# Graph attention, expert routing and a sparse feed-forward network on one core: routing moved into the graph attention's program, the bias in one product

## The reference

```python
x = x + gat(ctx, adj=layernorm(x))        # two layers, 8 heads of 64, weights W0, W1, biases b0, b1, elu
x = x + moe(layernorm(x))                 # logits = xn @ gate_w.T; top 2 of 8 experts, softmax of the two
x = x + cross_attention(layernorm(x), ctx)
x = x + ffn_2to4(layernorm(x))            # silu gate, 2048 wide, two of four kept, down
# in gat:
e = leaky_relu(attn_self + attn_neigh) + -1e10 * (1 - adj)
out = softmax(e) @ feat + b
```

## Time and profile before

| | us |
|---|---|
| median of 3 runs (lowest, highest) | 1199.75 (1198.94, 1200.93) |
| time of the profiled execution | 1200.97 |
| its span in the profile | 1199.3 |
| PE busy (share of the span) | 981.4 (82%) |
| DVE busy | 663.5 (55%) |
| ACT busy | 375.0 (31%) |
| POOL busy | 274.7 (23%) |

### The profile page before, as it was taken

One profiled execution on the slowest core, in us unless ns is written; L12 is line 12 of the kernel. 1 busy time (PEld: TensorE's weight loads), 2 busy tenths in 40 slices (PEclk: granted clock), 3 DMA queues, 4 the chain that ended last, 5 costly groups with the idle time before them and its releaser, 6 DMA issues. The chain is left out here.

```text
span 1199.3 us, 15555 instructions
## 1 busy us (share of the span) xinstructions
PE 981.4 (82%) x4555; PEld 812.4 (68%) x4556; DVE 663.5 (55%) x1384; ACT 375.0 (31%) x624; POOL 274.7 (23%) x299
## 2 busy tenths in 40 slices
PE   4967423999999997433357799999999999999996
PEld 3744203999999996322245678888888888888885
DVE  7955557442253422676788754454556555555445
ACT  5844311332343322333333411222122222212220
POOL 0466002333132510446613200301020100201000
PEclk8987655999999999576677999999999999999998
DMA  8357104454153521442101100201011100100001
GB/s 336 70 117 167 71 2 141 154 174 145 64 178 120 162 74 45 126 134 60 44 1 53 54 1 1 71 1 35 0 35 35 35 0 0 35 0 1 36 36 70
DMA packets 35836, 86.36 MB, mean 72 GB/s; under 512 B 5840, under 2 KB 5968, under 8 KB 34512
## 3 DMA queue, kind: packets, MB, share of 16 engines
q1 hardware_dynamic: 27216, 62.76, 14.9%
q0 software_dynamic: 8576, 23.08, 7.7%
HBM read 63.01 MB, written 22.81 MB: 72 GB/s over the span
## 5 line engine op out<-in xcount | busy, mean ns | idle before, releaser
L72 PE MATMUL ps<-f_x_lo,f_w_hi 128*128 128x512 f32 x512 | 202.8, 396 | 13.9 <-POOL f_w_lo L1131 7.2
L73 PE MATMUL ps<-f_x_hi,f_w_lo 128*128 128x512 f32 x512 | 201.6, 394 | 0.0
L74 PE MATMUL ps<-f_x_hi,f_w_hi 128*128 128x512 f32 x512 | 201.4, 393 | 0.0
L1193 DVE TENSOR_TENSOR f_hid<-f_sg,ps 128x512 f32<-128x512 f32 x64 | 43.8, 686 | 196.9 <-ACT f_sg L1188 196.7
L72 PEld LDWEIGHTS ps<-f_x_lo,f_w_hi 128*128 128x128 f32 x512 | 97.6, 191 | 35.7 <-DVE f_hid L1193 7.2
L74 PEld LDWEIGHTS ps<-f_x_hi,f_w_hi 128*128 128x128 f32 x512 | 97.5, 190 | 20.7
L73 PEld LDWEIGHTS ps<-f_x_hi,f_w_lo 128*128 128x128 f32 x512 | 97.7, 191 | 20.4
L72 PE MATMUL ps<-gu_w_lo,m_xT_hi 128*128 (+1 forms) x312 | 106.2, 340 | 4.0 <-DVE m_xT_lo L1651 3.1
L1188 ACT ACTIVATE f_sg<-ps 128x512 f32<-128x512 f32 x64 | 38.3, 599 | 227.6 <-PE ps L74 227.4
L72 PE MATMUL ps<-f_w_lo,kv_c_hi 128*128 128x512 f32 x256 | 102.1, 399 | 5.4 <-DVE x L2248 5.4
L73 PE MATMUL ps<-f_w_hi,kv_c_lo 128*128 128x512 f32 x256 | 101.9, 398 | 0.0
(11 more groups left out here) (303 smaller groups left out, 1939.9 us busy)
## 6 DMA issues: line engine op xcount, KB each, us to landing
raw<-in_moe_gu SPq DMA_DIRECT2D x32, 352.0 KB
y_scratch<-m_y SPq DMA_DIRECT2D x39, 256.0 KB
raw<-in_ffn_gu SPq DMA_DIRECT2D x16, 512.0 KB, 3.5
raw<-in_moe_dn SPq DMA_DIRECT2D x24, 256.0 KB
x<-in_x SPq DMA_DIRECT2D x4, 1024.0 KB, 12.7
gat_rows<-g_ybuf SPq DMA_DIRECT2D x16, 256.0 KB
xn_scratch<-g_n_xn SPq DMA_DIRECT2D x16, 256.0 KB, 2.3
raw<-in_ffn_dn SPq DMA_DIRECT2D x16, 256.0 KB, 2.6
```

The costliest lines, as they stand in the source:

```text
L72: eng.matmul(out, lhs_hi, rhs_lo, start=start, stop=False)
L73: eng.matmul(out, lhs_lo, rhs_hi, start=False, stop=False)
L74: return eng.matmul(out, lhs_hi, rhs_hi, start=False, stop=stop)
L1193: dve.tensor_tensor(out, sg[:, k, :], self.UP[k], ALU.mult).then_inc(self.hid_made, 1)
```

## The change

1. **The route block is gone.** A new class `Rank` does its work inside `gat_rows`: the choice of experts batch by batch as the logits arrive (`dve_choose`), the exponentials likewise (`act_exp`), the counts by small float32 products per batch (`pe_count`), then weights, places and one-hot matrices once (`dve_weights`, `dve_places`), the token half of the one-hot products' operand by ACT in 17 operations (`act_tokens`), the 32 products, now behind two halves of `off_hot` (`pe_index`), and the table by a compare and a transpose. Running sums over tiles, some clamps and copies are gone.
2. **The first four gathers** (`gather_rows`) come ahead of the barrier, on POOL.
3. **The logits** are made by one float32 product instead of `product3`; so the transposed tiles are only copied (ACT; DVE for batch 3), and `gate_w` isn't split. The copies go into `c_raw` and `w_raw` in turn, so they wait for the sums over these (`cmax_made`, `wsum_made`). `XN` is 8 buffers instead of 4.
4. **The order in `gat_rows`**: PE transposes batch 0 and 1 behind all `features`; `act_norm` of batch 0 comes at step 15; POOL has `pool_rstd(0)` ahead of `second_arg(3)`; all stores of normalised tiles come behind the rows' stores.
5. **The check's bounds** use the largest attention values as one factor: the Abs on ACT, `scale_w` on POOL and four loads of 256 KB are gone; `weight_sums` reads `w_raw`. The limits are `GAP_MIN` 65536 and `BOUND_MAX` 16000 instead of 16384 and 4000.
6. **The bias** of the second layer takes one product: its high part stands in row 0 and its low part in row 32 of one operand, and the stationary matrix has ones in both rows.
7. **In `moe`**, expert 0's weights are split as the other experts' are: ACT's four copies, DVE's four differences, then the down weights. The gathered rows, their indices and semaphores live outside `moe`, and later stages reuse the rows' space.

```diff
-                    pe.matmul(bank, first[:, :], b1_lo[:, :], start=True, stop=False)
-                    pe.matmul(bank, first[:, :], b1_hi[:, :], start=False, stop=False)
+                    pe.matmul(bank, first[:, :], b1_parts[:, :], start=True, stop=False)
...
-                        if b == B - 1 and m == 2:
-                            pe.wait_ge(pool_const, 3)
-                            for i in range(3):
-                                norm.pe_turn(pe, i)
-                        if b == B - 1 and m == 3:
-                            norm.pe_turn(pe, 3)
                         features(b, m)
...
+                turn_batch(0)
+                turn_batch(1)
                 pe.wait_ge(y_made, T)
                 lo.pe_logits(pe, 0)
                 lo.pe_turn_logits(pe, 0)
+                lo.pe_logits(pe, 1)
+                turn_batch(2)
+                lo.pe_turn_logits(pe, 1)
+                lo.pe_logits(pe, 2)
+                rank.pe_count(pe, 0)
...
+                turn_batch(3)
+                lo.pe_turn_logits(pe, 2)
+                lo.pe_logits(pe, 3)
+                rank.pe_count(pe, 1)
+                rank.pe_count(pe, 2)
+                lo.pe_turn_logits(pe, 3)
+                rank.pe_count(pe, 3)
+                rank.pe_index(pe)
...
# POOL
+                rank.pool_const(pool)
                 second_arg(0)
                 second_arg(1)
                 add_rows(0)
                 second_arg(2)
                 add_rows(1)
+                lo.pool_rstd(pool, 0)
                 second_arg(3)
-                scale_w(0)
-                norm.pool_rstd_for_act(pool, 0)
                 add_rows(2)
-                scale_w(1)
-                norm.pool_rstd_for_act(pool, 1)
+                lo.pool_rstd(pool, 1)
                 add_rows(3)
...
+                lo.pool_rstd(pool, 2)
+                lo.pool_rstd(pool, 3)
+                rank.pool_gather(pool)
...
# DVE, behind the loop's step 12
+                    if t == 13:
+                        dve.tensor_reduce(cmax[:, :], c_raw[:, :, :], AX.XY, ALU.max,
+                                          apply_absolute_value=True).then_inc(cmax_made, 1)
+                    if t in (12, 14):
+                        stats((t - 12) // 2)
...
                 for k in range(DC):
                     weight_sums(k)
+                weight_sums(DC).then_inc(wsum_made, 1)
+                stats(2)
...
                 lo.dve_logits(dve, 0)
+                rank.dve_choose(chain, 0)
+                stats(3)
                 lo.dve_logits(dve, 1)
+                rank.dve_choose(chain, 1)
                 for i in range(TB):
+                    lo.dve_copy(dve, 3 * TB + i)
                 lo.dve_logits(dve, 2)
+                rank.dve_choose(chain, 2)
...
                 lo.dve_logits(dve, 3)
+                rank.dve_choose(chain, 3)
+                rank.dve_weights(chain)
+                rank.dve_places(chain)
+                rank.dve_tokens(chain)
```

More of the change, by code:

```diff
@@ new lines, in dve_stats @@
+    def dve_stats(self, chain, c):
+        for i in range(TB):
+            ins = chain.eng.bn_stats(self.st[:, i, :], self.X[:, TB * c + i, :])
+        chain.link(ins)
+        for i in range(TB):
+            ins = chain.eng.bn_aggr(self.mv[:, TB * c + i, :], self.st[:, i, :])
+        chain.link(ins)
+        s = slice(TB * c, TB * c + TB)
+        chain.eng.tensor_scalar(self.ve[:, s], self.mv[:, s, 1], EPS, None, ALU.add).then_inc(self.var_ready, 1)
+        chain.eng.tensor_scalar(self.nmean[:, s], self.mv[:, s, 0], -1.0, None, ALU.mult).then_inc(self.var_ready, 1)
@@ L211, in act_norm @@
         if t >= self.XN:
+            act.wait_ge(self.turned, t - self.XN + 1)
             act.wait_ge(self.xn_stored[t % self.XN], 16 * (t // self.XN))
-        self.norm.act_norm(act, t)
-    def act_hi(self, act, t):
-        c, i = divmod(t, TB)
[L217 to L223, removed]
+        act.activation(self.xn[:, t % self.XN, :], self.X[:, t, :], ACT.Identity, bias=self.nmean[:, t:t + 1],
+                       scale=self.rstd[:, t:t + 1]).then_inc(self.xn_ready, 1)
@@ new lines, in pe_turn, with turned_tile @@
+    def pe_turn(self, pe, t):
+        bank = self.turn_banks[t % self.BANKS]
+        pe.wait_ge(self.xn_ready, t + 1)
+        if t >= self.BANKS:
+            pe.wait_ge(self.x_copied[(t - self.BANKS) // TB], (t - self.BANKS) % TB + 1)
+        for d in range(DC):
+            ins = pe.transpose(bank[:, P * d:P * d + P], self.xn[:, t % self.XN, P * d:P * d + P], self.ident[:, :])
+        ins.then_inc(self.turned, 1)
+    def turned_tile(self, eng, t):
+        c, i = divmod(t, TB)
+        eng.wait_ge(self.turned, t + 1)
+        if i == 0 and c >= 2:
+            eng.wait_ge(self.lg_done, c - 1)
+        return (self.x_t[c % 2][:, :, P * i:P * i + P],
+                self.turn_banks[t % self.BANKS].rearrange("p (d n) -> p d n", d=DC))
@@ L1415, in sb @@
             return ctx.enter_context(nc.sbuf_tensor("m_" + name, shape, dt))
[L1417 to L1419 removed]
+        rows, got = rt["rows"], rt["got"]
         xT_hi = sb("xT_hi", [P, 2, DC, P], F32R)
@@ L1635, in _ @@
                 act.sem_inc(y_done, 2)
+                split(0, slice(0, 1), range(DC))
                 rows_hi(0, 0)
+                act.wait_ge(ld_dn, 16 * RE)
+                act.copy(rt["dn_w_hi"][:, 0], rt["raw_dn"]).then_inc(dn_hi, 1)
                 act_silu(0, 0)
@@ L1720, in sb @@
             return ctx.enter_context(nc.sbuf_tensor("a_" + name, shape, dt))
-        pair = [sb(f"pair{k}", [P, D]) for k in range(2 * TB)]
+        pair = [rt["rows"][:, k, :] for k in range(TB)] + [sb(f"pair{k}", [P, D])[:, :] for k in range(TB)]
         x_hi = sb("x_hi", [P, 2, DC, N], F32R)
@@ L2293, in build @@
             "lg": sb("logits", [P, T, E]),
+            "rows": sb("moe_rows", [P, 4, D]),
+            "index": [sb(f"moe_index{k}", [P, 1], I32) for k in range(4)],
+            "spacer": sb("moe_spacer", [P, 1]),
+            "got": [sem(f"e_got{k}") for k in range(4)],
+            "index_ready": sem("e_index_ready"),
             "xn_dram": nc.dram_tensor("xn_scratch", (B * N, D), F32, kind="Internal").ap(),
```

691 lines of the change are left out of this document (347 added, 344 removed).

## The result

The changed kernel takes 1160.03 us (median of 4 runs, 1158.97 to 1162.02) against 1200.08 in the runs beside it: a ratio of 0.9669, interval 0.9652 to 0.9686. The forecast was 1161, range 1152 to 1176, so the total was met. Its terms were not all met, and two of the errors cancel. I compare the profiled executions, 1199.3 us of span before and 1160.3 after: 39.0 us less, where the sum said 38.4.

What follows compares the result with a forecast made beforehand. PE looked like the table loop's bound, beside a ring of ACT and DVE; the logits were a chain through all engines, routing DVE alone. -18.4 - 9.0 - 19.8 + 8.8 = -38.4 from 1199.75 gave 1161 us, range 1152 to 1176.

Steps and rivals of the forecast that it cites:

- The loop: Table loop until the last row tile: ends at 87.5 us instead of 105.9, by DVE's queue and the store; -18.4 us.
- Rival C: PE is the table loop's bound and its saving counts: up to 3.7 us more, 1158; within the likeliest case's 0.60.
- The logits: From the last row tile to the last logits: 41.5 us instead of 50.5, float32 products at 1.2 us each; -9.0 us.
- rival A: Logits and handover: warmer PE, float32 products at 0.9 us, and DVE not late behind the barrier; 1154 us, chance 0.15.
- rival B: POOL and its transfers set the pace: rstd of batches 1 to 3 and gathers later, 12 us lost; 1173, chance 0.20.
- The routing: From last logits to tokens: 16.5 us, replacing 36.3 of barrier and routing, tokens ready at 145.5; -19.8 us.
- The handover: From tokens to the first expert product: 15.8 us instead of 7.0, four uncovered gathers, then the barrier; +8.8 us.
- Behind the first product: From the first expert product to the kernel's end: unchanged at 999.6 us, later edits costed at nothing.

Runs made afterwards that it cites:

- bias_two: The changed kernel with the second layer's bias in two products again instead of one: 1161.25 us, ratio 0.9681 to the kernel before.
- abs_back2: The changed kernel with two Abs of 128x1024 put back on ACT, behind the squares of steps 1 and 2: 1161.56 us.
- late_pool: The changed kernel with the gathers behind the barrier, and POOL making one plain copy after the tokens, ahead of the barrier: 1152.89 us.
- one_ahead: The changed kernel with one gather ahead of the barrier and three behind it, instead of four ahead: 1155.01 us.
- landed_ahead: The changed kernel with all four gathers ahead of the barrier, and POOL waiting for them to land before it: 1161.17 us.

## Why the prediction was right, and where it wasn't

Each step is set against the profiled execution, with the last row's, logits' and tokens' ends as marks.

- **The loop, -18.4**: 86.0 instead of 87.5. The mechanism was right. DVE's queue behind the store ends it, in the order and nearly at the lengths that the working gave, and `bias_two` and `abs_back2` show that ACT's 2 us counted in full and PE's 3.7 hardly. Rival C falls. The store's wait was right as well (2.00 us). Of the 1.5 us, 1.2 stood already at `row(12)`, 78.3 for 79.5, and there the bias product was costed at nothing where `bias_two` shows 0.8.
- **The logits, -9.0**: the stretch takes 38.1 us instead of 41.5. The start (96.4 for 96.2) was right; the term that was mis-sized is the float32 product, 1.2 us where three batches of four take 0.90: 3.6 us. That is the first half of rival A. The clock of the earlier trace rows in this stretch, 0.70, was the wrong row to lean on: it is a mean over long waits, and in the new order PE hardly waits between the first and the last batch's products. The x rows landed 6 us behind the last issue of `add_rows(2)` (issue until 90.5, statistics at 96.51), where 3 was assumed; rival B's condition came true, but only 1.4 us of ACT's waiting came of it, ahead of the norms of batch 3.
- **The routing, -19.8**: 17.5 us behind the last logits instead of 16.5. DVE's own operations lasted what the earlier trace rows gave for their sizes (0.42 for 256 elements, 1.46, twice 2.28). The term that was mis-sized is the last counts: 1.7 us in the sum, 2.9 from `keep` (126.67) to the operation that reads them (129.57), of which DVE waits for 1.2. PE had fallen back to half its clock there, behind a wait of 2.9 us (granted 0.50 from 127.6 to 129.6), so the small products became the slower side:

```profile
127.61 1.43 PE L417 MATMUL ps<-g_keep,g_ones 128*128 128x24 f32 x6
...
129.57 0.29 DVE L436 TENSOR_TENSOR g_above<-ps,g_steps 128x128 f32<-128x128 f32 x1 [1.18 <-PE ps L421]
```

- **The handover, +8.8**: 20.2 us from tokens to the first product instead of 15.8, so +13.2. The four uncovered gathers (6.7) and the 4.1 us behind DVE's start were right. The step that failed is "barrier, flag and jump took ACT 2.2 us and DVE 4.99; they come now directly ahead of `moe`". That price was read where POOL had long been through. Move the last work onto POOL, and its DRAIN of 2.7 us, hidden in the kernel before, stands on the path, with 1.2 more behind a gather: 3.9. `late_pool` shows the first part alone, `one_ahead` that it does not grow with the number of gathers, `landed_ahead` that most of it isn't a wait for them to land. DVE's own lateness came again, as forecast; the second half of rival A did not happen.
- **Behind the first product, 999.6**: 998.5. The small edits there cost nothing. The profiles of the experiments on the changed kernel have between 996.4 and 998.7 in this part, so 1 us of it is no finding.

The errors are -1.5, -3.4, +1.0, +4.4 and -1.1: together -0.6. A total met to 0.1% therefore said little about the terms; a handover 4.4 us too cheap was paid by a product that was priced too dear.

The change as a whole gains 40 us and leaves some 10 more lying in one place, by moving four gathers ahead of a barrier that was cheap only while POOL came to it early. With the gathers behind it the kernel takes 1150.4 us.

## What to carry to other kernels

A barrier's price is not a constant: it is what the last engine to arrive still has to do. Before moving work in front of one, look at the sequencer's rows of the block's end on the engine that gets the work, even where they cost nothing now; on POOL, look above all in blocks in which it issues indirect transfers. Work that overlaps only itself ahead of a barrier may overlap the next stage's first copies behind it; here that was worth 9.6 us with the same instructions, of which 3.9 were POOL's DRAIN. And when the order in one queue is changed for another queue's sake, follow the next consumer: the new order alone won 18 us at the loop's end and kept 4.7.

## What the runs showed of the hardware

- POOL's DRAIN at the end of a block: in blocks in which POOL had issued indirect transfers, 2.7 us in the kernel before, 3.0 behind gathers that had landed, ending 2.7 behind a plain copy, and ending 3.7 to 4.1 us behind a gather just issued, one or four. In the two blocks of the kernel before in which POOL issued no transfer, it ended 0.1 us behind the last operation. DVE's, in the changed kernel, lasted 0.3 us.
- Behind a jump over long code DVE began 3.0 to 4.1 us later than ACT, and PE 3.0 to 4.5 in the kernels in which it did not wait for a gather; over a few instructions, all three began within 0.2 us.
- A float32 product of 512 columns with 8 output partitions took 0.90 us at 2.4 GHz and 1.20 at a mean clock of 0.74.
- One batch's indirect additions to `x` were seen landed 6.0 us behind their last issue (90.47 to 96.51), in a stretch in which the DMA engines were full (share 1.08 from 87.0 to 96.4).
